# A decoder layer on one core: how the 308 keys of a head group are divided for the attention's second product

## The chip, the cores and the metric

The program runs on one core of a Trainium2 chip. The metric is the time of one execution on the device, in microseconds; lower is better. TensorE does the matrix products and the transposes, and writes them to PSUM. ACT (ScalarE) and DVE (VectorE) read PSUM, POOL (GpSimd) works on SBUF alone, and SP issues the DMAs.

## The reference

Eight sequences of 512 tokens of width 512 pass a layer of three parts, each with a residual and a layer norm. The first mixes tokens with FFTs over the head dimension and a cumulative sum. The third is a linear layer with int4-rounded weights and a low-rank part. The change is in the second, cross-attention over 77 context keys:

```python
q = _split_heads(queries @ W_q + b_q)          # 16 heads of 32
k = _split_heads(keys @ W_k + b_k)
v = _split_heads(values @ W_v + b_v)
scores = jnp.einsum('bhqd,bhkd->bhqk', q, k) / jnp.sqrt(jnp.float32(d))
scores = jnp.where(mask == 0, jnp.float32(-1000000.0), scores)
attn = jax.nn.softmax(scores, axis=-1)
out = jnp.einsum('bhqk,bhkd->bhqd', attn, v)
return out @ W_o + b_o
```

All is float32. The kernel keeps that precision by splitting each operand x in a high part (x rounded to the type float32r) and the rest, and by adding three products: high times high, low times high, high times low.

## The kernel before

The program has three stages: weights are prepared, tokens are mixed for all eight batches, and `attend` does the attention and the last layer. `attend` is what the change touches.

**Heads in groups.** The 16 heads are taken as 4 groups (`GROUPS`) of 4 heads (`GH`). A group has 4 x 77 = 308 key columns (`GK`). `k_block` holds the keys of a group block-diagonally, so three matmuls give the scores of a group for 128 tokens: 128 rows (tokens) by 308 columns. `v_block` holds the values of a group in the same way: 308 rows by 128 columns. Since a product can contract at most 128 rows, the 308 are divided by `KC` in pieces of 103, 103 and 102.

**From scores to the second product.** For a tile of 128 tokens (t = 0 to 3), DVE masks the scores and finds the maxima (`softmax_top`), ACT takes the exponentials (`exponentials`), POOL multiplies with the inverse sums (`normalize_probs`). `turn_probs` transposes the result on TensorE: for each of the three pieces c, four transposes (one a group) into one PSUM bank, which is called P{t}{c}. `split_probs` on ACT copies the bank as high part to `pT_hi`, `split_probs` on DVE subtracts it from the bank and writes `pT_lo`, and frees the bank. `weigh_values` then does, for each group g, 3 pieces x 3 products = 9 matmuls of 512 columns (all tokens of the batch) into bank V{g}. It is written for a batch in the step of the next batch.

**Loading the values.** The values are computed in batch 0's step and go to DRAM (`values_split`, from `store_values`). `load_values` brings those of a batch back into `v_block`. `v_pieces` gives the parts: a head's 77 keys are cut where a piece of `KC` ends, so there are 6 parts, of 77, 26, 51, 52, 25 and 77 rows, each for the high and the low half: 12 DMAs of rows x 4 groups x 32 columns. POOL clears `v_block` once at the start.

**What sets the order.** Each engine runs an order written out by hand: the function `step` in each engine's part, a start (batch 0), a loop over batches 2 to 6 with step 1 before it, a step for batch 7 and one for what is left. A step scores batch i, weighs the values of batch i-1, then interleaves the output projection (O0 to O3), the FFN (T and F) of batch i-1, and the transposes and query projection (X and Q) of batch i+1. All of it but the scores shares four PSUM banks in a ring, in the order of `BANK_ORDER` (`START_ORDER`, `CLOSING_ORDER`, `END_ORDER` at the ends): a use waits until the one four places ahead is freed, which the semaphore `freed` counts. The functions named `split_x1`, `split_q`, `split_o`, `split_x2`, `split_v` split their banks as `split_probs` does. SP's queue, too, is in one order; in the start it is: two stores of values, `load_values(0)`, two stores, the keys of batch 1, the weights of the output projection and FFN, the last store, the residual of batch 1's first norm. The residual load waits until the last store of values has landed.

In the rows, `x_tok` is also the buffer of the residual (`res1`), and of the values before they are stored; `xT_and_qT` is shared by several tiles. L62 is the helper that issues the three products, L1345 the transposes of the probabilities, L1852 `split_probs` on DVE, L1574 on ACT, L1824 the splits of `split_o` and `split_q`, L1816 those of `split_x1` and `split_x2`, L1892 the adding of a residual, L1216 the value loads, L566 the key loads, L1237 the stores of values.

## Time and profile before

| | us |
|---|---|
| median of 3 runs | 952.46 |
| range of the runs | 952.28 to 957.01 |
| the profiled execution | 953.44 |
| its span in the trace | 951.6 |
| TensorE (PE) busy | 902.9 (95%) |
| weight loads (PEld) busy | 748.9 (79%) |
| DVE busy | 667.3 (70%) |
| ACT busy | 376.3 (40%) |
| POOL busy | 336.1 (35%) |

The attention part begins at about 463 us of the span. Busy time is that of an engine's instructions; a weight load overlaps the matmul before it. For matmuls, which are pipelined, the distance from start to start is the cost, not the length of the record. An idle time in brackets is what an instruction's engine stood still before it, with the name of what it waited for.

### The profile page before, as it was taken

The page shows a single profiled execution, that of the slowest core. Times are in us where ns is not written, and L with a number is a line of the kernel's source. Part 1 is how long each engine was busy: PE and PEld are TensorE (multiplying, and loading weights), DVE is VectorE, ACT ScalarE, POOL GpSimd, SP SyncE. Part 2 cuts the span into 40 slices and gives each one's busy share as a digit, 9 for nine tenths or more (in the row PEclk, how much of TensorE's full clock was granted, in tenths as well). Part 3 has the DMA queues.
Part 4 walks back from the last instruction along what each step waited for, and adds up shares of the span by engine and source line. Part 5 has one row for each costly group of instructions (what it writes and reads, how often), then busy time and mean ns, then how long its engine had stood idle before and what let it go on. Part 6 is the DMA issues. An engine that isn't in the chain of part 4 may idle for free.

```text
span 951.6 us, 14736 instructions
## 1 busy us (share of the span) xinstructions
PE 902.9 (95%) x4472; PEld 748.9 (79%) x4472; DVE 667.3 (70%) x1128; ACT 376.3 (40%) x1414; POOL 336.1 (35%) x312
## 2 busy tenths in 40 slices
PE   7847999999999999999699999999999999999997
PEld 7726888888888888888588888888888888888775
DVE  3762465666565666567666987979788797887957
ACT  5621211111111111101485656756567556666611
POOL 0230525252424342426421433314244151431703
PEclk9988999999999999999999999999999999999999
DMA  9795204040404121214747332220312214020021
GB/s 308 254 352 195 89 12 166 11 166 18 160 34 142 44 89 45 89 45 153 263 139 253 111 93 64 81 76 21 120 34 90 67 24 136 13 90 22 16 78 44
DMA packets 91996, 100.09 MB, mean 105 GB/s; under 512 B 42824, under 2 KB 49224, under 8 KB 91952
## 3 DMA queue, kind: packets, MB, share of 16 engines
q1 hardware_dynamic: 91951, 99.55, 31.8%
q8 instruction: 22, 0.36, 0.2%
q14 instruction: 23, 0.18, 0.1%
HBM read 60.50 MB, written 39.03 MB: 105 GB/s over the span
## 4 chain that ended last, share of the span: by engine, by line
PE 42%; DMA 3%; DVE 2%; POOL 2%; issue 1%; ACT 1%; SPq 0%; POOLq 0%; DVEq 0%
PE shared_ps L62 32%; PE score_ps L62 4%; PE shared_ps L1345 4%; PE shared_ps L1308 1%; DMA values_split<-x_tok 1%; PE shared_ps L1378 1%; POOL probs L1726 1%; DMA w_o_and_ffn<-weights_split 1%; DMA x_tok<-residual_between 1%; DVE x_and_res L1914 0%; DVE xT_and_qT L1816 0%; ACT probs L1567 0%; POOL x_and_res L1735 0%; DVE y L1892 0%; POOL rstd L1719 0%
## 5 line engine op out<-in xcount | busy, mean ns | idle before, releaser
L1567 ACT ACTIVATE probs<-score_ps,top_s 128x77 f32<-128x77 f32 x512 | 158.9, 360 | 27.9 <-DVE top_s L1873 27.7
L1726 POOL TENSOR_TENSOR probs<-probs,per_total 128x616 f32<-128x616 f32 x64 | 83.2, 1317 | 116.2 <-DVE per_total L1880 116.1
L1567 ACT ACTIVATION_READ_ACCUMULATOR probs<-score_ps,top_s 128x1 f32 x512 | 124.2, 243 | 0.0
L62 PE MATMUL shared_ps<-w_o_and_ffn,xT_and_qT 128*128 128x512 f32 x384 | 96.7, 400 | 4.5 <-DVE xT_and_qT L1816 3.8
L1719 POOL TENSOR_TENSOR rstd<-ve,half_power 128x1 f32<-128x1 f32 x64 | 42.2, 660 | 163.3 <-DVE ve L1903 158.8
L62 PE MATMUL shared_ps<-w_o_and_ffn,xT_hi 128*128 128x512 f32 x256 | 88.2, 407 | 2.1 <-DVE xT_lo L1824 1.8
L62 PEld LDWEIGHTS shared_ps<-w_o_and_ffn,xT_and_qT 128*128 128x128 f32 x384 | 70.1, 188 | 21.6 <-DVE xT_and_qT L1816 4.1
L840 POOL TENSOR_TENSOR mix_rstd<-mix_ve,half_power 128x1 f32<-128x1 f32 x32 | 22.1, 689 | 154.9 <-DVE mix_ve L971 154.9
L788 ACT ACTIVATE v_sb<-v_ps 128x512 f32<-128x512 f32 x32 | 18.6, 594 | 142.0 <-PE v_ps L62 142.0
L1574 ACT ACTIVATE pT_hi<-shared_ps 103x512 fp32r<-103x512 f32 (+1 forms) x96 | 54.6, 609 | 42.7 <-PE shared_ps L1345 42.1
L62 PE MATMUL out_ps<-w_back_hi,xT_and_qT 128*128 128x512 f32 x224 | 71.0, 398 | 0.0
L62 PE MATMUL score_ps<-xT_and_qT 128*128 128x308 f32 x384 | 64.8, 311 | 5.8 <-ACT probs L1567 3.9
L795 ACT ACTIVATE xT_and_qT<-vals 128x512 fp32r<-128x512 f32 x32 | 19.4, 631 | 126.0 <-POOL vals L849 110.2
L62 PEld LDWEIGHTS score_ps<-xT_and_qT 128*128 128x128 f32 x384 | 58.3, 191 | 9.1 <-ACT probs L1567 4.1
L1852 DVE TENSOR_TENSOR pT_lo<-shared_ps,pT_hi 103x512 fp32r<-103x512 f32 (+1 forms) x96 | 64.7, 685 | 0.2 <-ACT pT_hi L1574 0.2
L849 POOL TENSOR_TENSOR vals<-qs_prod 128x512 f32<-128x512 f32 x32 | 41.0, 1293 | 54.7 <-DVE qs_prod L952 54.7
L62 PEld LDWEIGHTS shared_ps<-w_o_and_ffn,xT_hi 128*128 128x128 f32 x256 | 48.9, 191 | 14.0 <-issue 2.8
L1868 DVE COPY_PREDICATED score_ps<-hidden,masked 128x616 f32<-128x616 int32 x64 | 56.4, 882 | 4.8 <-PE score_ps L62 4.5
L1735 POOL TENSOR_TENSOR x_and_res<-x_and_res,bias_f 128x512 f32<-128x512 f32 x32 | 42.2, 1320 | 36.5 <-DVE x_and_res L1914 23.7
L1345 PE MATMUL shared_ps<-ident,probs 128*103 128x128 f32 (+1 forms) x384 | 52.3, 273 | 1.9 <-POOL probs L1726 1.9
L1873 DVE TENSOR_REDUCE top_s<-score_ps 128x8 f32<-128x616 f32 x64 | 51.2, 800 | 3.6
L963 DVE TENSOR_TENSOR mix_r<-out_ps,x_res 128x512 f32<-128x512 f32 x29 | 20.1, 691 | 47.0 <-PE out_ps L62 47.0
(199 smaller groups left out, 2303.6 us busy)
## 6 DMA issues: line engine op xcount, KB each, us to landing
...
x_between<-mix_x SPq DMA_DIRECT2D x32, 256.0 KB, 2.1
residual_between<-mix_res SPq DMA_DIRECT2D x32, 256.0 KB, 2.1
...
out<-y_out SPq DMA_DIRECT2D x32, 256.0 KB, 2.0
...
```

What stands on the lines that cost most here:

```text
L62: last = nc.tensor.matmul(out, l, r, start=(n == 0), stop=(n == len(terms) - 1))
L840: nc.gpsimd.tensor_tensor(rstd[:, t % 2:t % 2 + 1], ve[:, t % 2:t % 2 + 1], half_power[:], ALU.pow).then_inc(rstd_ready, 1)
L849: nc.gpsimd.tensor_tensor(vals[:, h, :], qs[:, 2 * h, :], qs[:, 2 * h + 1, :], ALU.subtract if h else ALU.add).then_inc(vals_summed, 1)
L1345: last = nc.tensor.transpose(shared_ps[s.bank(use)][0:size, g * P:(g + 1) * P], probs[:, t % 2, g * GK + at:g * GK + at + size], ident[:])
L1567: nc.scalar.activation(probs[:, t % 2, j * KEYS:(j + 1) * KEYS], score_ps[:, g, k * KEYS:(k + 1) * KEYS], ACT.Exp, bias=top[:, t % 2, j:j ...
L1574: nc.scalar.activation(pT[0][0:size, c, :, t * P:(t + 1) * P], turned_bank(s, t, c), ACT.Copy).then_inc(turned_hi, 1)
L1719: nc.gpsimd.tensor_tensor(rstd[:, n:n + 1], ve[:, n:n + 1], half_power[:], ALU.pow).then_inc(rstd_ready, 1)
L1726: nc.gpsimd.tensor_tensor(p, p, per_total[:, t % 2, h * heads:(h + 1) * heads].unsqueeze(2) .to_broadcast([P, heads, KEYS]), ALU.mult).the ...
L1735: nc.gpsimd.tensor_tensor(res2[:, t % 2, :], x2[:, t % 2, :], bias_f[:], ALU.add).then_inc(res2_ready, 1)
L1852: nc.vector.tensor_tensor(pT[1][0:size, c, :, tok], turned_bank(s, t, c), pT[0][0:size, c, :, tok].bitcast(F32), ALU.subtract).then_inc(fr ...
L1868: nc.vector.copy_predicated(s4, hidden[:, t, :].unsqueeze(1).unsqueeze(1).to_broadcast(shape), masked[:].unsqueeze(1).unsqueeze(1).to_broa ...
L1873: nc.vector.tensor_reduce(top[:, t % 2, h * 8:(h + 1) * 8].rearrange("p (g j) -> p g j", j=GH), s4, AX.X, ALU.max, negate=True).then_inc(t ...
```

## The change

The pieces of a group become 122, 122 and 64. In groups 0 and 2 the 64 are the last columns (244 to 307), in groups 1 and 3 the first (0 to 63). So the 64 of group 0 and the 64 of group 1 are neighbours in `probs`, and one transpose of 128 columns turns both: the rows 0 to 63 of its result belong to the even group, the rows 64 to 127 to the odd one. `turn_probs` has four transposes in the first bank (both 122s of groups 0 and 1) and four in the second (those of groups 2 and 3), and two in the third.

In the third bank ACT copies the high parts of the even and of the odd groups in two instructions, each to its own 64 rows of a new tile `pT_tail`. DVE writes the low parts, again in two instructions, to the other 64 rows of the same group's column block. So `pT_tail[:, g]` has the high part in one half of its rows and the low part in the other. `v_tail[0]` has the high part of the values in both halves, `v_tail[1]` the low part only beside the high part of the probabilities. Two products then do what three did. The two DVE instructions count on a semaphore of their own, `tail_lo`; DVE waits for both and adds one to `freed` itself.

The value loads follow: `v_pieces` has 10 parts (77, 45, 32, 77, 13 rows for the even groups, 13, 77, 32, 45, 77 for the odd ones), each for two of the four groups, for high and low half, and three DMAs of 64 rows for each parity fill `v_tail`: 26 in place of 12.

```diff
-KC = [(0, 103), (103, 103), (206, 102)]
+TAIL = 64
+CHUNK = (GK - TAIL) // 2
+
+MAIN = [[0, CHUNK], [TAIL, TAIL + CHUNK]]
...
-    for j in range(GH):
-        for c, (at, size) in enumerate(KC):
-            a, b = max(j * KEYS, at), min((j + 1) * KEYS, at + size)
-            if a < b:
-                yield j, c, a - at, a - j * KEYS, b - a
+    for odd in range(2):
+        for j in range(GH):
+            for c, at in enumerate(MAIN[odd]):
+                a, b = max(j * KEYS, at), min((j + 1) * KEYS, at + CHUNK)
+                if a < b:
+                    yield odd, j, c, a - at, a - j * KEYS, b - a
+
+
+V_LOADS = 2 * len(list(v_pieces())) + 6
...
             def load_values(i):
 
                 wait_reuse(sp, oT_hi, i * NC)
+                src = [v_dram[part].rearrange("r (g j d) -> r g j d", g=GROUPS, j=GH) for part in range(2)]
                 for part in range(2):
-                    src = v_dram[part].rearrange("r (g j d) -> r g j d", g=GROUPS, j=GH)
-                    for j, c, row, key, n in v_pieces():
-                        sp.dma_start(v_block[part][row:row + n, c, :, j * XHD:(j + 1) * XHD].bitcast(F32),
-                                     src[bass.ds(i * KEYS + key, n)][:, :, j, :]).then_inc(v_loaded, 16)
+                    for odd, j, c, row, key, n in v_pieces():
+                        sp.dma_start(v_block[part][row:row + n, c, odd:GROUPS:2, j * XHD:(j + 1) * XHD].bitcast(F32),
+                                     src[part][bass.ds(i * KEYS + key, n)][:, odd:GROUPS:2, j, :]).then_inc(v_loaded, 16)
+                for odd, j, key in ((0, GH - 1, KEYS - TAIL), (1, 0, 0)):
+                    for part, half in ((0, 0), (0, 1), (1, odd)):
+                        sp.dma_start(v_tail[part][64 * half:64 * (half + 1), odd:GROUPS:2, j * XHD:(j + 1) * XHD].bitcast(F32),
+                                     src[part][bass.ds(i * KEYS + key, TAIL)][:, odd:GROUPS:2, j, :]).then_inc(v_loaded, 16)
...
-            sp.wait_ge(values_cleared, 2)
+            sp.wait_ge(values_cleared, 4)
...
-                at, size = KC[c]
-                for g in range(GROUPS):
-                    last = nc.tensor.transpose(shared_ps[s.bank(use)][0:size, g * P:(g + 1) * P],
-                                               probs[:, t % 2, g * GK + at:g * GK + at + size], ident[:])
+                if c < 2:
+                    for k in range(2):
+                        for g in range(2):
+                            at = (2 * c + g) * GK + MAIN[g][k]
+                            last = nc.tensor.transpose(shared_ps[s.bank(use)][0:CHUNK, (2 * k + g) * P:(2 * k + g + 1) * P],
+                                                       probs[:, t % 2, at:at + CHUNK], ident[:])
+                else:
+                    for k in range(2):
+                        at = (2 * k + 1) * GK - TAIL
+                        last = nc.tensor.transpose(shared_ps[s.bank(use)][:, k * P:(k + 1) * P],
+                                                   probs[:, t % 2, at:at + 2 * TAIL], ident[:])
...
+                out = shared_ps[s.bank(use)][:]
+                terms = [(v_block[a][:, c, g, :], pT[b][:, c, g, :]) for c in range(2) for a, b in ((0, 0), (1, 0), (0, 1))]
+                for n, (l, r) in enumerate(terms):
+                    nc.tensor.matmul(out, l, r, start=(n == 0), stop=False)
+
+                nc.tensor.matmul(out, v_tail[0][:, g, :], pT_tail[:, g, :], start=False, stop=False)
+                nc.tensor.matmul(out, v_tail[1][:, g, :], pT_tail[:, g, :], start=False, stop=True).then_inc(filled, 1)
...
+                    psum, (hi, lo) = turned_main(s, t, c)
+                    nc.scalar.activation(hi, psum, ACT.Copy).then_inc(turned_hi, 1)
...
+                else:
+                    for odd in range(2):
+                        psum, (hi, lo) = turned_tail(s, t, odd)
+                        nc.scalar.activation(hi, psum, ACT.Copy).then_inc(turned_hi, 1)
...
+                    dve.wait_ge(turned_hi, nth(i, NT * 4, 4 * t + 3))
+                    psum, (hi, lo) = turned_tail(s, t, 0)
+                    nc.vector.tensor_tensor(lo, psum, hi.bitcast(F32), ALU.subtract).then_inc(tail_lo, 1)
+                    psum, (hi, lo) = turned_tail(s, t, 1)
+                    nc.vector.tensor_tensor(lo, psum, hi.bitcast(F32), ALU.subtract).then_inc(tail_lo, 1)
+                    dve.wait_ge(tail_lo, nth(i, NT * 2, 2 * t + 1))
+                    dve.sem_inc(freed, 1)
```

**SP, start of the attention part: `load_values(0)` and the stores after it.** In the names, `values_split` is the DRAM buffer; rows x groups x columns. Before:

```order
L1216 DMA v_block_hi<-values_split 77x4x32 [waits x1_stored1,v_stored0,v_stored1,x1_stored0,values_cleared]
L1216 DMA v_block_hi<-values_split 26x4x32
L1216 DMA v_block_hi<-values_split 51x4x32
L1216 DMA v_block_hi<-values_split 52x4x32
L1216 DMA v_block_hi<-values_split 25x4x32
L1216 DMA v_block_hi<-values_split 77x4x32
```

and the same six for the low half. Of the change:

```order
L1231 DMA v_block_hi<-values_split 77x2x32 [waits x1_stored1,v_stored0,v_stored1,x1_stored0,values_cleared]
L1231 DMA v_block_hi<-values_split 45x2x32
L1231 DMA v_block_hi<-values_split 32x2x32
L1231 DMA v_block_hi<-values_split 77x2x32
L1231 DMA v_block_hi<-values_split 13x2x32 x2
L1231 DMA v_block_hi<-values_split 77x2x32
L1231 DMA v_block_hi<-values_split 32x2x32
L1231 DMA v_block_hi<-values_split 45x2x32
L1231 DMA v_block_hi<-values_split 77x2x32
L1235 DMA v_tail_hi<-values_split 64x2x32 x2
L1235 DMA v_tail_lo<-values_split 64x2x32
```

The ten of `v_block` come again for the low half, the three of `v_tail` for the odd groups. Twelve issues have become 26; behind them, unmoved, follow the stores, keys, weights and the residual.

**DVE, in a step, around the split of token tile 0's third bank, up to the next maxima.** `stats`, `mv` and `ve` belong to the layer norm, `top_s` to the softmax. Before:

```order
L1901 BN_AGGR mv<-stats 128x2 [waits stat_done]
L1903 TENSOR_SCALAR ve<-mv 128x1 [waits aggr_done]
L1852 TENSOR_TENSOR pT_lo<-shared_ps,pT_hi 102x4x128 [waits pT_hi_ready]
L1868 COPY_PREDICATED score_ps<-hidden,masked 128x2x308 [waits scored,hidden_ready]
L1873 TENSOR_REDUCE top_s<-score_ps 128x8 [waits exped,hid]
```

Of the change:

```order
L1942 BN_AGGR mv<-stats 128x2 [waits stat_done]
L1944 TENSOR_SCALAR ve<-mv 128x1 [waits aggr_done]
L1890 TENSOR_TENSOR pT_tail<-shared_ps,pT_tail 64x2x128 [waits pT_hi_ready]
L1892 TENSOR_TENSOR pT_tail<-shared_ps,pT_tail 64x2x128
L1909 COPY_PREDICATED score_ps<-hidden,masked 128x2x308 [waits tail_lo,scored,hidden_ready]
L1914 TENSOR_REDUCE top_s<-score_ps 128x8 [waits exped,hid]
```

One instruction of 512 columns has become two of 256 with fewer rows, and what stands behind them waits for them (`tail_lo`).

**TensorE, `weigh_values` of one group.** Before, nine matmuls, three times:

```order
L62 MATMUL shared_ps<-pT_hi,v_block_hi 128x512 [waits pT_hi_ready,shared_freed,v_loaded]
L62 MATMUL shared_ps<-pT_hi,v_block_lo 128x512
L62 MATMUL shared_ps<-pT_lo,v_block_hi 128x512
```

Of the change, the like of these twice (L1385), and then:

```order
L1387 MATMUL shared_ps<-pT_tail,v_tail_hi 128x512
L1388 MATMUL shared_ps<-pT_tail,v_tail_lo 128x512
```

Nothing else on TensorE moves, but the third transposes of each tile, of which two are left of four.

## Rows read from the trace of the kernel before

**Rows 1.** One stretch of an ordinary step: length, busy us and instructions, PEclk, DMA.
```profile
626.50:685.00 58.50, 57.93 (x311) 49.23 (x310) 48.90 (x91) 35.35 (x156) 20.48 (x20) 1.00 0.23 67
```

**Rows 2.** Waits of the weight loads, 440 to 952: total us, times, longest.
```profile
PEld shared_ps L1345 <- DVE xT_lo L1816: 0.9, 5, 0.2
```

**Rows 3.** Timeline of TensorE and DVE in that step: start, us, instruction, [idle before].
```profile
650.53 3.06 PE L62 MATMUL shared_ps<-w_o_and_ffn,xT_and_qT 128*128 128x512 f32 x12 [0.57 <-DVE xT_and_qT L1816]
663.44 0.65 PE L1345 MATMUL shared_ps<-ident,probs 128*102 128x128 f32 x4
...
648.28 0.69 DVE L1892 TENSOR_TENSOR y<-shared_ps,x_tok 128x512 f32<-128x512 f32 x1
...
662.09 1.29 DVE L1816 TENSOR_TENSOR xT_lo<-shared_ps,xT_hi 128x512 fp32r<-128x512 f32 x2
```

**Rows 4.** The chain that ended last, 460 to 545: start, us, what.
```profile
509.39 11.19 DMA values_split<-x_tok
...
520.59 5.59 DMA x_tok<-residual_between
...
534.18 3.04 PE shared_ps L62 x12
```

**Rows 5.** Timeline of SP's queue in the start.
```profile
487.56 5.29 SPq L1216 DMA_DIRECT2D v_block_hi<-values_split  x6
...
497.99 2.75 SPq L1237 DMA_DIRECT2D values_split<-x_tok  x4
500.79 3.82 SPq L566 DMA_DIRECT2D xT_and_qT<-keys_split  x8
```

**Rows 6.** Timeline of TensorE: end of the values, first output projection, last transposes.
```profile
636.81 0.39 PE L62 MATMUL shared_ps<-pT_lo,v_block_hi 102*128 102x512 f32 x1
637.04 1.86 PE L62 MATMUL score_ps<-xT_and_qT 128*128 128x308 f32 x12
638.84 0.49 PE L62 MATMUL shared_ps<-w_o_and_ffn,xT_hi 128*128 128x512 f32 x1
...
681.25 1.47 PE L1345 MATMUL shared_ps<-ident,probs 128*103 128x128 f32 x12
682.47 0.48 PE L62 MATMUL shared_ps<-xT_hi,w_q_hi 128*128 128x512 f32 x1
```

**Rows 7.** Timeline of ACT and DVE: the splits of the weighed values.
```profile
636.13 0.80 ACT L1580 ACTIVATE xT_hi<-shared_ps,bias_v 128x512 fp32r<-128x512 f32 x1
637.24 0.69 ACT L1580 ACTIVATE xT_hi<-shared_ps,bias_v 128x512 fp32r<-128x512 f32 x1 [0.30 <-PE shared_ps L62]
...
637.96 0.75 DVE L1824 SCALAR_TENSOR_TENSOR xT_lo<-shared_ps,bias_v,xT_hi 128x512 fp32r<-128x512 f32 x1 [0.24 <-ACT xT_hi L1580]
```

**Rows 8.** Groups by form: busy us, mean ns of one; last, a wait for itself.
```profile
L1852 DVE TENSOR_TENSOR pT_lo<-shared_ps,pT_hi 102x512 fp32r<-102x512 f32 x32 | 21.8, 682 | 0.0
...
L440 DVE TENSOR_TENSOR xT_and_qT<-side,xT_and_qT 128x208 fp32r<-128x208 f32 x2 | 0.7, 366 | 0.0
...
L474 DVE TENSOR_TENSOR xT_and_qT<-turned,xT_and_qT 16x512 fp32r<-16x512 f32 x1 | 0.7, 683 | 0.0
...
643.84 0.18 DVE L1901 BATCH_NORM_AGGREGATE mv<-stats 128x2 f32<-128x6 f32 x1 [0.16 <-DVE stats L1898]
```

**Rows 9.** Single value loads (51, 52, 77 rows), and us of a store to landing.
```profile
489.50 0.76 SPq L1216 DMA_DIRECT2D v_block_hi<-values_split  x1
...
490.31 0.85 SPq L1216 DMA_DIRECT2D v_block_hi<-values_split  x1
...
492.02 0.83 SPq L1216 DMA_DIRECT2D v_block_hi<-values_split  x1
...
values_split<-x_tok SPq DMA_DIRECT2D x8, 256.0 KB, 2.2
```

**Rows 10.** Timeline of TensorE: first score and first output projection of step 1.
```profile
510.11 1.01 PE L62 MATMUL score_ps<-xT_and_qT 128*128 128x308 f32 x6
...
522.11 0.47 PE L62 MATMUL shared_ps<-w_o_and_ffn,xT_hi 128*128 128x512 f32 x1 [0.16 <-issue]
```

39 lines of the change are left out of this document (20 added, 19 removed).

## The prediction

> **What bounds the kernel now.** I read the stretches first, then the waits, then single engines in order of time. In one ordinary batch step of the attention part TensorE is busy 57.93 of 58.50 us at a granted clock of 1.00, and DVE 48.90 [rows 1]. So a matmul less should be time less. Two things qualify this. In each step TensorE stops once for 0.57 us before the FFN of the first token tile, and DVE is what it waits for [rows 3]. And a little later there is a place without slack: over the loop, the weight load of the transposes P12 (probabilities of token tile 1, third bank) waits for DVE's `xT_lo` five times, 0.9 us in sum [rows 2]. Between the two DVE runs in one piece: it begins at 648.28, when the third output projection is filled, and the pair of `xT_lo` that releases P12 starts at 662.09 and takes 1.29; TensorE starts P12 at 663.44 [rows 3]. That is 15.2 us of a step in which DVE sets the pace and TensorE only follows. In the rest of the step TensorE does.
>
> At the start of the attention part the bound is another one. The chain of waits goes through the DMAs: the last store of values is issued at 509.39 and lands 11.19 us later, behind the weights; the load of the residual for the first output projection follows at 520.58 and takes 5.59; DVE adds it, and that ends in the FFN matmuls at 534.18 [rows 4]. Ahead of it SP issues without a pause: two times six value loads, four stores, eight key loads [rows 5]. Whatever is put into that row of issues moves the residual.
>
> **TensorE: what is removed.** Per token tile 12 transposes become 10. Twelve take from 681.25 to the next product at 682.47, 1.22 us, so 0.10 each [rows 6]; 0.20 per tile. Per group of values 9 matmuls become 8. V3's last matmul starts at 636.81 and the score behind it at 637.04 [rows 6]: 0.23 each, 0.92 per batch. A batch gives 4 x 0.20 + 0.92 = 1.72 us on TensorE, eight batches 13.8.
>
> **How much of the 0.92 arrives.** After V3 TensorE does two scores (637.04) and starts the output projection at 638.84 [rows 6], since it needs V3 split. ACT is in the way: its split of V2 starts at 636.13, as soon as the exponentials are through, and V3's at 637.24, having waited 0.30 for TensorE [rows 7]. With V3 done 0.92 earlier, at 636.3, ACT is still at exponentials and V2. These start earlier only by the one matmul that V0 and V1 are each shorter (about 0.2), so ACT takes V3 at about 636.6 and DVE, 0.67 apart from V2's, ends at 638.2 in place of 638.7 (it starts at 637.96 and takes 0.75 [rows 7]). The output projection moves by 0.50 and the other 0.42 are waited.
>
> **DVE: what is added.** The third piece of a tile was one TENSOR_TENSOR of 682 ns [rows 8]; now it is two of 64x256, which the rows do not have. 128x208 takes 366 and 16x512, as few rows as that, 683 [rows 8], so rows do not count and columns do: 48 more columns at (682 - 366) / 304 = 1.04 ns make 416. Back to back a record overlaps the next by 0.09, so the pair costs 0.65 where one cost 0.59: +0.07. Then DVE waits for its own results and adds one to `freed`. The same pattern (wait on itself, then an increment) stands in the norm: aggregate waits 0.16 idle for stats [rows 8], and the overlap of 0.09 is lost too: +0.25. Bounds are 0.04 and 0.35; I take 0.25, as the pattern is the same. Sum +0.32 per tile. Queued behind that wait are the masking of the next scores (tile 0), a split of queries, a norm. For tile 0 it stands inside the 15.2 us, so all of it arrives at P12: +0.32. For tiles 1 and 2 DVE has over 0.5 us in hand where TensorE needs it next. For tile 3 it comes just ahead of the next batch's V0, where 0.1 is lost. ACT's pair of halves is about as much dearer (+0.07) but ACT sits idle next to each.
>
> **Sum of an ordinary step.** Tile 0's transposes: 0, since TensorE waits for DVE there anyway (0.57 becomes 0.77). P12 late +0.32. Tiles 1, 2, 3: -0.60. V0 +0.10. V part -0.50. Sum -0.68. Other waits have little slack too (the bank for the last query projection), for which I allow 0.15, an estimate of a quarter of the gain: **-0.53 per step** instead of -1.72. Cover: what hides nothing is TensorE's; if DVE were not on the chain, the whole 1.72 came out.
>
> **SP: the added issues.** A batch's values come in 26 DMAs, not 12. Two times six took 487.56 to 497.99, 10.43 us, 0.87 each with the gap [rows 5]. Their issue takes 0.83 for 77 rows, 0.85 for 52 and 0.76 for 51 [rows 9]; key loads of 32 rows, with the same three-level pattern, take 3.82 us for eight, 0.48 apart [rows 5]. Which price do the new shapes have? Of the 26, sixteen have 77, 45 or 13 rows, ten have 32 or 64. I price the sixteen like the old value loads (0.87) and the ten like key loads (0.48), as they are nearest by rows: 13.9 + 4.8 = **18.7 us, +8.3**. Ends: all at 0.48 (the pattern now has 2 groups in place of 4) 12.5, +2.1; all at 0.87 22.6, +12.2.
> By the Trainium skill, page "DMA: Bandwidth & Descriptors", section "Why a DMA increments its semaphore by 16 and not by 1", a transfer runs on the largest number of DMA engines up to 16 that divides its slowest dimension, and the sequencer itself writes the semaphore counts of the rest. By that rule 32 and 64 rows fall in with the key loads and 45 and 13 do not, which is my split; the trace agrees in that 32 rows go 0.48 apart and 77 and 52 rows take 0.83 and 0.85, but 51 rows, by the rule those with the most to write, take 0.76.
>
> In an ordinary step this hides: TensorE reads the values a step later, and the output store queued behind waits for nothing that DVE needs before the third tile. In batch 0 it does not hide. SP has 0.95 us in hand there (four stores take 2.75 [rows 5], four issues of 0.45 would take 1.8), so keys and weights go 7.35 later. Before them, ACT's split of the last values needs the third store landed: issued at 506.8 in the new order, 2.2 to land [rows 9], 509.0. From there follow that split, two more banks (together 2.9, an estimate from splits of 0.6 to 0.7 by ACT and DVE each [rows 7, 8], partly side by side) and the last query projection (12 x 0.23 = 2.8): the first score of step 1 starts at 514.7 in place of 510.11 [rows 10]. That would cost 4.6, but the other path is later: weights issued at 512.0, last store of values landed at 527.9, residual at 533.5 in place of 526.18 [rows 4]. From its landing to the FFN DVE is busy in one piece, so TensorE reaches the FFN at 541.5 instead of 534.18: **+7.35**. What batch 0 and V of batch 1 save before that is waited away.
>
> **Sum.** Start +7.35. Rest of step 1: +0.32 - 0.60 + 0.25 = -0.03. Steps 2 to 7: 6 x -0.53 = -3.18. Last step: V alone, without exponentials in ACT's way, -0.92. Total +3.2. The profiled execution took 953.44 (span 951.6), 0.98 over the median of the three runs; so 956.6 against its own time, and against the median, 952.46, 955.7. What a measurement here can tell from no change is about 0.5%, 4.8 us: below 947.7 or above 957.2.
>
> **The rivals.** (1) *TensorE alone sets the steps*, DVE gives way: the waits at P12 are only 0.9 us in five [rows 2], so some slack might appear there, and the DVE stretch holds instructions slowed by neighbours. Then step 1 gives -0.60 and six steps 1.72 each, the last 0.92: 7.35 - 0.6 - 10.3 - 0.9 = -4.5, 948.0. Against it: DVE has no idle row between 648.28 and 662.09 beyond waits for itself. (2) *Cheap issues*: half as many runs per DMA make all 26 cost 0.48: start +1.1 (2.1 less 0.95), total -3.0, 949.5. With (1) as well, -10.7, 941.8. (3) *Slower than before*: the issues of the value loads ahead of the residual. If the 32- and 64-row loads cost 0.87 as well, the start costs 11.25 and the total is +7.1, 959.6. The place is SP's row of issues in batch 0, the price 0.39 more for ten issues; it decides from about 20 us for the 26 issues on. (4) *The change does not do what it says*: halves at other partitions, or a wait dearer than in the norm, cost DVE 0.7 more per step in its stretch: a step gives +0.17, step 1 +0.67, total +8.1, 960.6.
>
> **Chances.** Forecast 0.42 (own range 953 to 958.5); (1) 0.17; (2) 0.13; (1) and (2) together 0.03; (3) 0.17; (4) 0.08. The 80% range reaches from rival 1 to (3) and (4): 946.5 to 961. Faster by over 0.5%: half of rival 1 and the joint case, with what noise adds, 0.13. Slower by over 0.5%: (3), (4) and a quarter of the forecast, 0.35. The same: 0.52.
>
> **What would show it.** Right: SP's first batch of value loads takes 18 to 19 us; 32- and 64-row loads are short issues and 45- and 13-row ones long; the residual lands about 7 us later and DVE's first add of an output projection waits 4 or more for it; a step's period is about 57.8 in place of 58.4 (the first output projections of steps 1 and 3 start at 522.11 and 638.84, 116.73 apart for two steps [rows 6, 10]); the wait before the first FFN tile grows from 0.57 to about 0.8; the halves take about 416 ns. Wrong in the steps: a period under 57.2 (rival 1) or over 58.5 (4). Wrong at the start: issues done in under 15 or over 21 us.

## The result and the profile after

| | median | runs | ratio to before |
|---|---|---|---|
| before | 953.22 us | 6 (952.28 to 957.01) | |
| after | 966.61 us | 6 (964.59 to 967.71) | 1.0133, 95% [1.0113, 1.0153] |
| predicted | 955.7 us | range 946.5 to 961.0 | |

The change makes the kernel 1.3% slower, 12.7 us by the ratio. The forecast was +3.2; the sign of its likeliest case was right, the size was not, and the time lies outside the range. The profiled execution of after took 967.71 us.

In the page of after TensorE is busy 4 us less and DVE 13 us more (667.3 in the page of before), over a span 14 us longer:

```profile
span 965.9 us, 14884 instructions
...
PE 898.9 (93%) x4376; PEld 737.6 (76%) x4376; DVE 680.7 (70%) x1160; ACT 381.2 (39%) x1446; POOL 330.0 (34%) x314
```

**The start.** SP's queue in the changed kernel, the place of [rows 5] (start, us, instruction). L1231 and L1235 are the value loads of the main chunks and of the tails:

```profile
490.57 8.73 SPq L1231 DMA_DIRECT2D v_block_hi<-values_split  x10
499.34 8.23 SPq L1231 DMA_DIRECT2D v_block_lo<-values_split  x10
507.62 1.24 SPq L1235 DMA_DIRECT2D v_tail_hi<-values_split  x2
...
511.49 2.06 SPq L1256 DMA_DIRECT2D values_split<-x_tok  x4
513.59 3.84 SPq L573 DMA_DIRECT2D xT_and_qT<-keys_split  x8
```

The 26 loads take 20.9 us where twelve took 10.43 [rows 5]. The chain behind them is the one of [rows 4], moved as a whole (chain of waits; start, us, what; the last line is DVE's add, from its timeline):

```profile
522.25 11.24 DMA values_split<-x_tok
533.50 5.47 DMA x_tok<-residual_between
539.07 0.70 DVE y L1933
```

From the landing of the residual to the first FFN tile it takes 8.0 us in both. That tile starts at 546.96 instead of 534.18 [rows 4]. The +12.8 divides into 3.0 by which the loads begin later (chance, as K shows below), 10.5 for their issue, and 0.7 that the four stores behind them (2.06 against 2.75) give back. So 9.8 of it belong to the change.

**The steps.** The first FFN tile of steps 2 and 3, and P12, the third-bank transposes of token tile 1 (timeline of TensorE; the first row ends with its window, inside the tile):

```profile
604.82 2.37 PE L69 MATMUL shared_ps<-w_o_and_ffn,xT_and_qT 128*128 128x512 f32 x9 [0.79 <-DVE xT_and_qT L1850]
...
663.10 3.06 PE L69 MATMUL shared_ps<-w_o_and_ffn,xT_and_qT 128*128 128x512 f32 x12 [0.78 <-DVE xT_and_qT L1850]
...
676.72 0.44 PE L1371 MATMUL shared_ps<-ident,probs 128*128 128x128 f32 x2
```

The two FFN tiles are 58.28 apart, as in the kernel before. So TensorE's saving of 1.7 us a step is gone whole. In this step TensorE is busy 56.7 of the 58.3 us, in the kernel before 57.7, so 1.0 of it stands there as idle time; the rest is in gaps that this sum doesn't show. For the stretch 590 to 840, the waits of TensorE in the changed kernel (total us, times, longest), where before has only the first of these with 2.9 us:

```profile
PE shared_ps L69 <- DVE xT_and_qT L1850: 3.9, 5, 0.8
PE shared_ps L69 <- DVE xT_lo L1858: 1.4, 5, 0.3
PE shared_ps L69 <- DVE y L1933: 1.1, 4, 0.3
PE shared_ps L1385 <- DVEq L1894: 0.8, 4, 0.2
```

All four releasers are on DVE; the last is the line with the increment behind DVE's wait on itself. And what DVE does there (its timeline, tile 0):

```profile
663.93 0.15 DVE L1944 TENSOR_SCALAR ve<-mv 128x1 f32<-128x1 f32 x1
664.12 0.42 DVE L1890 TENSOR_TENSOR pT_tail<-shared_ps,pT_tail 64x256 fp32r<-64x256 f32 x1
664.57 0.43 DVE L1892 TENSOR_TENSOR pT_tail<-shared_ps,pT_tail 64x256 fp32r<-64x256 f32 x1
665.37 0.81 DVE L1909 COPY_PREDICATED score_ps<-hidden,masked 128x616 f32<-128x616 int32 x1 [0.37 <-DVE pT_tail L1892]
```

From `ve` to the mask it is 1.44 us. In the kernel before the same two stand 0.71 apart:

```profile
651.38 0.15 DVE L1903 TENSOR_SCALAR ve<-mv 128x1 f32<-128x1 f32 x1
651.48 0.69 DVE L1852 TENSOR_TENSOR pT_lo<-shared_ps,pT_hi 102x512 fp32r<-102x512 f32 x1
652.09 0.80 DVE L1868 COPY_PREDICATED score_ps<-hidden,masked 128x616 f32<-128x616 int32 x1
```

### The profile page after: what moved, and what is told of

It reads as the page before. It is cut to its first block, busy times and chain, and to the rows that moved or that the text cites. A ratio compares the mean times of both kernels' runs of the same rounds, so it can differ in the third digit from the quotient of the medians.

```text
span 965.9 us, 14884 instructions
## 1 busy us (share of the span) xinstructions
PE 898.9 (93%) x4376; PEld 737.6 (76%) x4376; DVE 680.7 (70%) x1160; ACT 381.2 (39%) x1446; POOL 330.0 (34%) x314
## 4 chain that ended last, share of the span: by engine, by line
PE 29%; DVE 8%; ACT 4%; issue 4%; SPq 3%; DMA 3%; DVEq 0%; POOLq 0%; POOL 0%; ACTq 0%
PE shared_ps L69 22%; ACT probs L1597 3%; PE score_ps L69 2%; SPq L1231 2%; DMA values_split<-x_tok 1%; PE shared_ps L1366 1%; DVE score_ps L1909 1%; DVE y L1933 1%; PE shared_ps L1327 1%; DVE stats L1939 1%; DMA w_o_and_ffn<-weights_split 1%; PE shared_ps L1408 1%; ACT xT_hi L1614 1%; PE shared_ps L1385 1%; DVE xT_lo L1858 1%
## 5 line engine op out<-in xcount | busy, mean ns | idle before, releaser
L1753 POOL TENSOR_TENSOR rstd<-ve,half_power 128x1 f32<-128x1 f32 x64 | 38.4, 600 | 166.0 <-DVE ve L1944 165.9
L69 PEld LDWEIGHTS score_ps<-xT_and_qT 128*128 128x128 f32 x384 | 58.1, 190 | 10.4 <-ACT probs L1597 5.5
L1909 DVE COPY_PREDICATED score_ps<-hidden,masked 128x616 f32<-128x616 int32 x64 | 59.6, 931 | 6.2 <-PE score_ps L69 3.6
L1605 ACT ACTIVATE pT_hi<-shared_ps 122x512 fp32r<-122x512 f32 x64 | 37.1, 615 | 39.6 <-PE shared_ps L1366 38.7
L69 PE MATMUL shared_ps<-w_o_and_ffn,xT_lo 128*128 128x512 f32 x128 | 50.7, 396 | 0.0
L69 PEld LDWEIGHTS out_ps<-w_back_hi,xT_and_qT 128*128 128x128 f32 x224 | 41.6, 188 | 9.6
```

Source lines behind the costliest of these rows:

```text
L69: last = nc.tensor.matmul(out, l, r, start=(n == 0), stop=(n == len(terms) - 1))
L1605: nc.scalar.activation(hi, psum, ACT.Copy).then_inc(turned_hi, 1)
L1753: nc.gpsimd.tensor_tensor(rstd[:, n:n + 1], ve[:, n:n + 1], half_power[:], ALU.pow).then_inc(rstd_ready, 1)
L1909: nc.vector.copy_predicated(s4, hidden[:, t, :].unsqueeze(1).unsqueeze(1).to_broadcast(shape), masked[:].unsqueeze(1).unsqueeze(1).to_broa ...
```

## The experiments

All times are medians beside runs of before on the same chip (953.4 to 954.7); the ratio has its 95% interval. "Period" is the distance from one step's first FFN tile to the next one's in the profile, the typical one of steps 2 to 6. In the kernel before it is 58.28, in the changed kernel 58.28.

| kernel | us | ratio | period |
|---|---|---|---|
| K before again | 954.2 | 1.0008 [0.9990, 1.0026] | 58.26 |
| A 12 more issues, batch 0 | 963.7 | 1.0087 [1.0058, 1.0115] | 58.23 |
| E 12 more issues, later batches | 953.8 | 1.0007 [0.9995, 1.0020] | 58.22 |
| B after, start reordered | 961.4 | 1.0059 [1.0038, 1.0080] | 58.34 |
| R after, 14 loads | 957.3 | 1.0038 [1.0020, 1.0056] | 58.29 |
| D TensorE's saving alone | 948.2 | 0.9920 [0.9897, 0.9942] | 57.12 |
| H DVE's halves and wait alone | 957.6 | 1.0048 [1.0029, 1.0066] | 58.79 |
| P both | 951.1 | 0.9970 [0.9953, 0.9987] | 57.74 |
| Q P and ACT's halves | 949.5 | 0.9959 [0.9944, 0.9973] | 57.75 |
| T1 Q, halves on different rows | 952.4 | 0.9989 [0.9966, 1.0012] | 57.97 |
| T2 T1, results moved to other rows | 954.7 | 1.0008 [0.9992, 1.0025] | 58.17 |
| C after without the wait | 964.3 | 1.0102 [1.0083, 1.0122] | 57.94 |
| G unstacked, 64-row matmuls | 971.9 | 1.0204 [1.0176, 1.0231] | 59.04 |
| GB G, start reordered | 970.3 | 1.0180 [1.0161, 1.0200] | 59.03 |
| M unstacked, 128-row matmuls | 960.6 | 1.0089 [1.0063, 1.0115] | 57.58 |
| N M with 12 loads | 951.5 | 0.9973 [0.9958, 0.9988] | 57.60 |
| S N, start shortened | 950.7 | 0.9970 [0.9954, 0.9986] | 57.56 |

### The start

**A, E.** `load_values` of before, each load in two; in A for batch 0, in E for all others:

```
-sp.dma_start(v_block[part][row:row + n, c, :, j * XHD:(j + 1) * XHD].bitcast(F32),
-             src[bass.ds(i * KEYS + key, n)][:, :, j, :]).then_inc(v_loaded, 16)
+for odd in range(2) if isinstance(i, int) and i == 0 else [None]:
+    groups = slice(0, GROUPS) if odd is None else slice(odd, GROUPS, 2)
+    sp.dma_start(v_block[part][row:row + n, c, groups, j * XHD:(j + 1) * XHD].bitcast(F32),
+                 src[bass.ds(i * KEYS + key, n)][:, groups, j, :]).then_inc(v_loaded, 16)
```

> The kernel before with one thing changed: each of the 12 value loads of batch 0, ahead of step 1, is cut in two (groups 0 and 2, groups 1 and 3), the same bytes in 24 loads. Theory SP (the loss of the change is the time that SyncE takes to issue loads at the start, 0.82 to 0.87 us for each whatever its rows): 12 more issues x 0.83 = +10.0, less some 0.7 of slack, so +9 us in all, 962 us; the residual lands 10 us later, and the first FFN tile starts 9 us later. Rival (a halved load is issued in 0.44 us, as the 64-column ones of the tails suggest): +5.3 - 0.7 = +4.6. Rival (the loss is DVE's and the stacking's, the start's issues are hidden): 0.

> The kernel before with the value loads of batches 1 to 7 cut in two (24 instead of 12) and those of batch 0 left whole, the counterpart of A_start_issues. Theory (in the steps SyncE is idle most of the time, its issues lie beside the rest): within 1 us of before, 953 to 954.5, period 58.3. Rival (every issue costs, for instance since the next batch's keys and the stores stand behind them): up to +9 us a step.

A: +9.0 us by the medians (8.3 by the ratio), as the SP theory said. Its queue (x12 are the loads of one half):

```profile
490.84 10.30 SPq L1218 DMA_DIRECT2D v_block_hi<-values_split  x12
501.19 10.09 SPq L1218 DMA_DIRECT2D v_block_lo<-values_split  x12
```

E: no difference. Twelve more loads cost 9.0 us together, 0.75 each, where the next thing waits for them, and nothing in a step.

**R.** With high and low rows side by side in DRAM one load fetches both; 14 loads instead of 26, the rest as in the changed kernel:

```
-    v_dram = nc.dram_tensor("values_split", (2, B * KEYS, D), F32).ap()
+    v_dram = nc.dram_tensor("values_split", (B * KEYS, 2, D), F32).ap()
...
-                src = [v_dram[part].rearrange("r (g j d) -> r g j d", g=GROUPS, j=GH) for part in range(2)]
+                src = v_dram.rearrange("r a (g j d) -> r (a g) j d", g=GROUPS, j=GH)
```

> The changed kernel with the high and low values of a key side by side in DRAM, so that one load fetches both: 14 value loads a batch instead of 26, everything else as in the changed kernel, stacking and wait too. Theory (of the changed kernel's 12 to 13 us, 9 are the start's issues and the rest the end and chance): the start's loads take 11.5 us, 9 us less than in the changed kernel, and the whole is at 956 to 959, 3 to 5 us over before, with a period of 58.3. Rival (the start's delay comes from the stacked tiles, not from the issues): 965.

957.3, inside what was expected. The stacking, the wait and the period are those of the changed kernel, and 9.1 us of its loss (by the ratios) are gone. So about 9 of the 12.7 us are the issues of twelve loads at the start; R still has two more than the kernel before.

**B.** The order of SP's start:

```
-                sp.wait_ge(v_stored[n], 32)
-            load_values(0)
+            sp.wait_ge(v_stored[0], 32)
+            load_values(0, 0)
             store_values(2)
+            load_values(0, 1)
             store_values(3)
+            load_values(0, 2)
             load_next_keys(1)
+            store_values(4)
```

The second argument says which part (high, low, tails). Behind it come `w_o`, the residual, then `w_ffn`.

> The changed kernel with SyncE's start in another order: batch 0's values need the first stored tile alone, so its loads begin behind that store, and the stores of tiles 2, 3 and 4 are issued as soon as their tile is split instead of behind all 26 value loads; the residual goes ahead of the FFN weights. Nothing else differs. Theory SP: the 6.0 us in which TensorE waited for the split of tile 3, whose slot the late store held, and the late residual go: some 9 to 11 us below the changed kernel, 956 to 958 us; what is left over 953 is the end of the program. Rival (the stacked steps themselves cost more, DVE): at most 2 us less than the changed kernel, 965.

5.2 us less than the changed kernel by the medians, 7 by the ratios, where 9 to 11 were expected. The late store is no longer waited for (6.0 us in the changed kernel), but the keys of batch 1, which stand behind the same loads, are (waits of TensorE, 440 to 962; total us, times, longest):

```profile
PE score_ps L69 <- DMA xT_and_qT<-keys_split: 3.8, 1, 3.8
```

The queue is full from 484 to 518 us. An order can choose who waits; only fewer or cheaper issues shorten it.

**K.** The 3.0 us by which the loads of after began late:

> The kernel before, unchanged, for a second profile of it. The changed kernel's value loads of batch 0 began 3.0 us later than in the first profile of before (490.6 against 487.6), though nothing ahead of them was changed. Theory (that 3.0 us is chance, of the matmuls on the context at a lower granted clock): the loads begin at 490 to 491 here too, the first FFN tile of step 1 at 537, the period of a step is 58.3. Rival (the change itself delays them): they begin at 487.6 again. Ratio 1.00.

K's loads began at 487.05, as the rival had it, and yet the change isn't what delays them: A, which is the kernel before up to that point, began at 490.84. Over all profiles with this order of the start, in the eleven of the kernel before and kernels made from it they began at 487.05 to 491.57 (mean 489.0), in the six of the changed kernel and kernels made from it at 487.29 to 491.06 (mean 489.1). So the delay comes and goes without the change. Where it comes, TensorE has waited longer for the loads of the first value product (2.94 us in A, 1.69 in K), and the granted clock is then down for a part of the stretch to the lower of its two levels, 1.2 GHz: that product takes 4.57 in A, 3.02 in K. A and then K (start and end, length, TensorE busy, clock, DMA share, GB/s):

```profile
475.00:480.00 5.00, 2.74 (x7) 0.72 0.97 352
```

```profile
475.00:480.00 5.00, 5.00 (x30) 1.00 0.84 294
```

**F.** Behind the end of the kernel before, loads of eleven shapes, one at a time (one run, 1024.5 us with them):

```
+            sp.dma_start(spare[0:77], v_dram[0].rearrange("r (g j d) -> r g j d", g=GROUPS, j=GH)[0:77, :, 0]).then_inc(spare_loaded, 16)
+            sp.wait_ge(spare_loaded, 16)
```

> The kernel before, and behind its end 33 further loads of parts of the stored values into a spare tile, one at a time, each behind the landing of the one before: eleven shapes, each three times (77, 80, 128, 64, 32, 16 and 13 rows, with 4 runs or 2 runs of 32 columns a row, and 77 rows with one run of 128 columns). It tells what the 0.82 to 0.87 us of a value load's issue, the 0.60 of a tail's and the 0.48 of a key's go with. Theory (a load has one price whatever its rows, but 64 rows are divided among the 16 engines without a rest): 64, 80, 128, 32 and 16 rows at 0.6, 77, 45 and 13 rows at 0.83. Rival (the price goes with the count of runs): 77x4 the dearest, 16x4 and 13x2 under 0.5. The program is some 70 us longer by it.

One of the three turns, in the order 77 rows x 4 runs, 45 x 2, 32 x 2, 13 x 2, 80 x 4, 16 x 4, and 77 rows with one run of 128 columns (min/median/max ns):

```profile
L1300 SPq DMA_DIRECT2D spare<-values_split x1: 848/848/848, 951.0 to 951.0; - x1
...
L1304 SPq DMA_DIRECT2D spare<-values_split x1: 849/849/849, 955.7 to 955.7; - x1
...
L1306 SPq DMA_DIRECT2D spare<-values_split x1: 647/647/647, 958.0 to 958.0; - x1
...
L1308 SPq DMA_DIRECT2D spare<-values_split x1: 849/849/849, 960.0 to 960.0; - x1
...
L1314 SPq DMA_DIRECT2D spare<-values_split x1: 599/599/599, 966.3 to 966.3; - x1
...
L1318 SPq DMA_DIRECT2D spare<-values_split x1: 599/599/599, 970.8 to 970.8; - x1
...
L1320 SPq DMA_DIRECT2D spare<-values_split x1: 350/350/350, 972.7 to 972.7; - x1
```

Rows that 16 divides are issued in 0.56 to 0.65 us, the others of this run in 0.82 to 0.86, 80 rows cheaper than 77 and 77 as dear as 13, as the theory said; the number of runs hardly matters until the row is one run, which costs 0.32 to 0.35. Sixteen loads of the dear kind (0.84), ten of the cheap one (0.61) and 0.04 between two make 20.6 of the changed kernel's 20.9 us.

By the Trainium skill, page "DMA: Bandwidth & Descriptors", section "Why a DMA increments its semaphore by 16 and not by 1", a transfer runs on the largest number of DMA engines up to 16 that divides its slowest dimension, here the rows, and the sequencer writes the semaphore counts of the others. The two prices fall as that division does. But the counts left over don't order the dear ones: 45 rows, which leave one by that rule, take 0.85 to 0.88 in the changed kernel (once 1.09), 25 and 51 rows, which leave 11 and 13, take 0.76 to 0.77 in the kernel before. What the 0.2 us between the two kinds are is open.

### The steps

**D.** In `turn_probs` and `weigh_values` of before:

```
-                for g in range(GROUPS):
+                for g in range(GROUPS if c < 2 else 2):
...
+                terms = [(l[a], r[b]) for l, r in pieces for a, b in ((0, 0), (1, 0), (0, 1))][:8]
```

> The kernel before with TensorE's saving alone: of the third bank only two of the four transposes are made, and of each value bank the last of the nine matmuls is left out, so part of the attention is left out; DVE, ACT and the loads are as before. Theory (the chain DVE to ACT to TensorE sets the value part, TensorE sets the rest): the 8 transposes give 0.6 per step and the value part 0.1 to 0.4 of its 0.92: 0.7 to 1.0 a step, 5 to 8 us in all, 945 to 948. Rival (TensorE alone sets the steps): 1.7 a step and 0.9 in the last, 13 us in all, 940. Rival (DVE alone sets them): 0 to 1 us.

-6.5 us and 1.16 a step, a little more of a step than expected. TensorE alone doesn't set the steps (1.7 was there to be had), but two thirds of its saving arrive when DVE is left as it is. The changed kernel has the same saving and a period of 58.28; it loses 1.16 against D. The next runs divide that.

**H, P, Q.** On DVE, and in Q in the same way on ACT:

```
+for k in range(2):
+    nc.vector.tensor_tensor(pT[1][0:size, c, 2 * k:2 * k + 2, tok], turned_bank(s, t, c)[:, 2 * k:2 * k + 2],
+                            pT[0][0:size, c, 2 * k:2 * k + 2, tok].bitcast(F32),
+                            ALU.subtract).then_inc(half_lo, 1)
+dve.wait_ge(half_lo, nth(i, NT * 2, 2 * t + 1))
+dve.sem_inc(freed, 1)
```

> The kernel before with DVE's part of the change alone: the low part of the third bank is made in two halves of 256 columns (102 rows each), behind them DVE waits for both and only then frees the bank; matmuls, ACT and loads are as before. Theory (the halves and the wait take back what TensorE gives, 1.15 us a step by the periods of 58.27 in the changed kernel and 57.12 with TensorE's saving alone): +0.8 to +1.2 a step, +6 to +9 us in all, 961 to 963. Rival (the step's end is set by TensorE in other stretches, so DVE's loss shows only where TensorE's gain is): 0 to +2 us, 955 to 957. The prediction's own term was +0.32 a step, +2.5 us.

> The kernel before with TensorE's saving (D_pe_only: two transposes of the third bank and one matmul of each value bank left out) and DVE's part (H_dve_only: two halves, a wait, then the free) together; ACT and the loads as before. D alone gave a period of 57.12, H alone 58.79, before has 58.28. Theory (with TensorE faster the DVE halves cost more than the 0.51 they cost alone, since DVE now sets the value part as well; they account for nearly all that the changed kernel loses against D): 58.0 to 58.3, 952 to 955. Rival (the costs are plain sums, and the rest of the changed kernel's loss is ACT's halves): 57.6, 949.

> P_pe_and_dve with ACT's part added: the high part of the third bank is made in two operations of 256 columns as well, and DVE's first half waits for both, as in the changed kernel; two transposes and a value matmul in nine are left out as there. Theory (ACT's second half makes DVE's halves, and with them the exponentials and the value part, later: the 0.53 us a step that is left of the changed kernel's loss against D_pe_only): a period of 58.1 to 58.3, 3 to 4 us above P_pe_and_dve, 954 to 955. Rival (ACT is idle there and the 0.53 comes from the 122-row transposes and banks): 57.75, 951.

H: +0.51 a step, half of what I expected then, 0.2 more than the prediction's term. P: +0.62 on top of D. It lies between its two answers and near the second: the costs are nearly plain sums. Q: nothing, so ACT's halves cost nothing and that theory fell. 0.53 a step stayed open.

**C.** The changed kernel, each half frees the bank itself and such a bank counts as two:

```
-    dve.wait_ge(tail_lo, nth(i, NT * 2, 2 * t + 1))
-    dve.sem_inc(freed, 1)
...
+    return sum(2 if u[0] == "P" and u[2] == "2" else 1 for u in uses)
```

> The changed kernel without DVE's wait on itself behind the two halves of the tail: each half frees the bank by itself, and the counts of freed banks are two for such a bank. Theory (the wait holds DVE's sequencer, so that the mask operation behind it starts 0.37 us late and later waits are not met ahead): 0.25 to 0.37 us less for each of the 4 tiles on DVE, of which the periods show 0.5 per step: 3 to 4 us below the changed kernel, 962.5 to 963.5. Rival (DVE's wait lies beside other work): the same time, 966.5.

0.34 less a step (0.5 was expected), and in all 2.3 us less by the medians, 3.0 by the ratios, at or under the low end of the range. The wait costs 0.35 on DVE, 1.09 from `ve` to the mask instead of 1.44:

```profile
661.93 0.15 DVE L1950 TENSOR_SCALAR ve<-mv 128x1 f32<-128x1 f32 x1
662.11 0.87 DVE L1900 TENSOR_TENSOR pT_tail<-shared_ps,pT_tail 64x256 fp32r<-64x256 f32 x2
663.02 0.81 DVE L1915 COPY_PREDICATED score_ps<-hidden,masked 128x616 f32<-128x616 int32 x1
```

Of the 0.34, 0.32 arrive at P12 (13.30 behind the first FFN tile instead of 13.62).

**T1, T2.** In Q the halves have 102 rows each, all read from row 0 on. In the changed kernel the second is read from row 64 on, and both are written to the other 64 rows. T1 gives Q's halves rows 0 to 63 and 64 to 101; T2 also writes them to the other half:

```
-for k, rows, to in ((0, slice(0, 64), slice(0, 64)),
-                    (1, slice(64, size), slice(64, size))):
+for k, rows, to in ((0, slice(0, 64), slice(64, 128)),
+                    (1, slice(64, size), slice(0, size - 64))):
```

> Q_pe_dve_act with DVE's two halves cut to 64 and 38 rows, written to the rows that they are read from; the rest of the low part is left as it is, so part of the attention is left out. Control for T2. Theory (the count of rows doesn't matter to DVE, only the columns): as Q_pe_dve_act, two halves in 0.75 us, a period of 57.75, 949 to 951.

> T1_rows_kept with the results written to the other half of the rows (rows 0 to 63 to 64 to 127, rows 64 to 101 to 0 to 37), as the changed kernel's stacking does. Theory (a result that moves to other rows can't overlap with the operation before or behind it): the halves take 0.42 us each and start at least 0.03 behind the end of the one before, 0.2 us more for each tile, a period of 58.1 to 58.3, 3 to 4 us above T1. Rival (the 0.53 is the changed kernel's own tiles and banks, the tail's tile shared by ACT and DVE for one): as T1, 57.75.

T1's theory fell: it isn't Q's time, but 0.22 a step more. T2 adds another 0.20, a period inside its theory's range; in time it adds 2.4 us by the medians, less than the 3 to 4 expected. The two from `ve` on, Q and then T2 (T2's second half has 38 rows; a merged row shows the shape of its first):

```profile
650.72 0.15 DVE L1917 TENSOR_SCALAR ve<-mv 128x1 f32<-128x1 f32 x1
650.82 0.75 DVE L1863 TENSOR_TENSOR pT_lo<-shared_ps,pT_hi 102x256 fp32r<-102x256 f32 x2
651.94 0.81 DVE L1882 COPY_PREDICATED score_ps<-hidden,masked 128x616 f32<-128x616 int32 x1 [0.37 <-DVE pT_lo L1863]
```

```profile
658.03 0.15 DVE L1918 TENSOR_SCALAR ve<-mv 128x1 f32<-128x1 f32 x1
658.22 0.87 DVE L1864 TENSOR_TENSOR pT_lo<-shared_ps,pT_hi 64x256 fp32r<-64x256 f32 x2
659.46 0.81 DVE L1883 COPY_PREDICATED score_ps<-hidden,masked 128x616 f32<-128x616 int32 x1 [0.37 <-DVE pT_lo L1864]
```

In Q the first half starts 0.10 behind the start of `ve`, which takes 0.15: they overlap. In T2 it starts when `ve` is over. The way from `ve` to the mask is 0.71 in before, 1.22 in Q, 1.35 in T1, 1.43 in T2, 1.44 in the changed kernel. So of its +0.73, 0.51 are two halves and the wait, 0.13 the second half on other rows than the first, 0.08 the results on other rows than the sources. The rows of Q divide the 0.51: the pair takes 0.75 where one operation took 0.69, DVE then stands idle 0.37, and the 0.08 by which the mask overlapped the operation before it are lost. T1's first half has 64 rows and takes the same 0.42 as Q's 102, so it isn't the count of rows. TensorE meets this at two places of a step: from Q to T2 P12 starts 0.19 later behind the first FFN tile (13.42 and 13.61), and V0 0.24 later behind the score ahead of it (0.95 and 1.19), which is how 0.21 on DVE becomes 0.42 in the period. By the Trainium skill, page "VectorE: DVE Perf Modes", section "Two Vector instructions with no wait between them", a DVE instruction is held until all earlier ones have finished when its first row lies in another group of 32 than that of the last read, or of the last write, in the same memory. That names in Q none, in T1 the second half, in T2 and the changed kernel both; the trace agrees, at about 0.1 us each.

### What the stacking is good for, and a faster kernel

**G, GB.** The shared transposes without the stacking: one ACT and one DVE operation of 128 rows x 256 columns for the tail bank, high and low in tiles of their own, and for each group

```
-nc.tensor.matmul(out, v_tail[0][:, g, :], pT_tail[:, g, :], start=False, stop=False)
-nc.tensor.matmul(out, v_tail[1][:, g, :], pT_tail[:, g, :], start=False, stop=True).then_inc(filled, 1)
+rows = slice(64 * (g % 2), 64 * (g % 2 + 1))
+for a, b in ((0, 0), (1, 0), (0, 1)):
+    last = nc.tensor.matmul(out, v_tail[a][rows, g, :], pT_tail[b][rows, g // 2, :], start=False, stop=(b == 1))
```

> The changed kernel with the shared transposes of the 64s but without the stacking: the tail bank (128 rows, 256 columns) is split by one ACT operation into a high tile and by one DVE operation into a low tile, and each group's value bank takes three matmuls on its own 64 rows (9 in all, as before), 24 value loads instead of 26. Theory (stacking costs DVE more than its one matmul saves): DVE has 256 columns less per tile than before and no wait on itself, TensorE keeps the 8 transposes' saving, 0.6 a step: a period of 57.3 to 57.7, 4 to 7 us below the changed kernel in the steps and 1 us in the start, 959 to 962. Rival (TensorE's ninth matmul costs what the stack saved): period 58.2, 965.

> The same with SyncE's start in the other order (values of batch 0 behind the first store, later stores between the pieces, residual ahead of the FFN weights). Theory: both gains add, 5 us below G_unstacked, 954 to 957, about the kernel before or a little under. Rival (the start of step 1 is held by the 24 loads whatever their order): as G_unstacked.

Both were far off: 971.9 and 970.3. The way to the values was D's (V0 34.95 behind the first FFN tile, D 34.88), but the value part took 10.7 us instead of 9.1. TensorE in the first value bank (L1384 the 122-row matmuls, L1388 the 64-row ones):

```profile
697.10 0.39 PE L1384 MATMUL shared_ps<-pT_lo,v_block_hi 122*128 122x512 f32 x1
697.42 0.49 PE L1388 MATMUL shared_ps<-pT_tail_hi,v_tail_hi 64*128 64x512 f32 x1
697.76 0.39 PE L1388 MATMUL shared_ps<-pT_tail_hi,v_tail_lo 64*128 64x512 f32 x1
697.99 0.39 PE L1388 MATMUL shared_ps<-pT_tail_lo,v_tail_hi 64*128 64x512 f32 x1
698.31 1.12 PE L69 MATMUL score_ps<-xT_and_qT 128*128 128x308 f32 x6
```

Matmuls of one size start 0.23 apart. Where 122 rows turn to 64, the starts are 0.32 and then 0.34 apart: 0.2 more for each such change, two changes a bank, eight a batch: the 1.6 us.

**M.** The same three matmuls on all 128 rows, with zeros for the other group's values.

> G_unstacked with one thing changed: the three tail matmuls of each value bank contract all 128 rows, against values that are zero in the other group's half, instead of the group's own 64 rows. Theory (in G_unstacked each change between a 122-row and a 64-row matmul cost TensorE 0.1 us on both sides of it, 0.39 us per bank, 1.5 us a step): the value part is 9.1 us again, the period 57.5 to 57.7, 10 us below G_unstacked, 961 to 963, of which 8 to 9 over before are the 24 loads at the start and 4 to 5 under it the steps. Rival (that extra time is the wait for the tail's low part, whose rows come late): as G_unstacked, 972.

960.6, 11.4 us below G, the period 57.58: confirmed. The stacking avoids the same price by filling the 128 rows, but so do zeros, and then DVE needs one operation, no move and no wait.

**N, S.** M with R's layout, 12 loads; S also with one store for each tile's high and low values and a shorter start.

> M_padded with the high and low values of a key side by side in DRAM, so that one load fetches both: 12 value loads instead of 24, each with 4 runs of 32 columns a row. Theory (the issue price is per load, 0.83 us, whatever its columns): the start's loads take 10 us as in the kernel before, the first FFN tile starts where it does there, 533 to 537, and with a period of 57.5 to 57.7 the kernel is at 948 to 950, 4 to 5 us below before. Rival (the price goes with the bytes or runs of a load): the loads take 18 us and the time stays at M_padded's.

> N_padded_12_loads with SyncE's start shortened: one store for each tile's high and low values instead of two, batch 0's loads behind the first store alone, the last store ahead of the weights and the residual ahead of the FFN weights. Theory (the start of step 1 is still held by SyncE's queue: 2.5 us of waiting for w_o and the late residual in N_padded_12_loads): 2 to 4 us below it, 947 to 949.5. Rival (the rest of the start is set by ACT and TensorE): the same as N_padded_12_loads, 951.

N: 951.5, ratio 0.9973, a gain over before that the runs can tell, though smaller than expected: its loads take 10.4 us as in before, but of the 4 to 5 us that 0.7 a step should give only 2 to 3 are there. In its profile the steps give 3.3 and the last two 0.6, and the loads begin 3.5 us later than in before, by the chance that K shows; what the other executions lost was not divided. S isn't told apart from N. Its residual is issued 13.4 us earlier (510.67 against 524.08), and still the first FFN tile starts only 1.8 earlier. The wait for weights that its expectation meant to remove (2.5 in N, 2.8 in S) is that of the first value product, at 474 to 477, ahead of all value loads, as in before (1.7), and not one for `w_o`.

## Why the prediction was wrong

- **The start, +7.35: right in its mechanism, too small.** The chain was the one foretold: loads, last store, residual, DVE's add, FFN. The split into sixteen dear and ten cheap loads was right. The term that failed is the price of the ten: 0.48 apart, taken from the key loads, where the trace has 0.64 to 0.68 (0.60 to 0.64 each and the gap). With some dear ones over 0.87 too that is 20.9 us instead of 18.7. The slack behind was 0.7, not 0.95. So the start costs 9.8 instead of 7.35; twelve loads alone measured +9.0 (A) and, taken out, -9.1 (R). Rival 3, all 26 at 0.87 and a start of +11.25, was nearer, 1.5 too high where the forecast was 2.4 too low.
- **DVE, +0.32 a tile: this step failed.** The two halves and the wait cost 0.51, not 0.32 (Q). The pair's +0.07 was right (0.06). The wait, +0.25 with the lost overlap and taken from the norm (0.16 idle), was not: DVE stands idle 0.37 and loses 0.08 of overlap, 0.45 together, over the upper of its two bounds. What makes the norm's wait cheaper was not tested. The sentence that rows do not count is right for how long an operation takes and wrong for when it can start: the halves lie on other rows than their neighbours and than their own sources, which costs 0.2 more. Together +0.73 on DVE. Of this +0.71 arrive at P12: it starts 13.62 behind the first FFN tile, against 12.91 [rows 3].
- **Tile 3, "0.1 is lost": too small.** V0 starts 1.21 behind the score ahead of it, against 0.85 before: +0.36. TensorE waits 0.20 of it by name, for DVE.
- **The value part, -0.50: right.** From V0 to the first output projection it takes 10.47, before 10.93: -0.46. The output projection waits 0.28 for `xT_lo`.
- **The transposes of tiles 1 to 3, -0.60: right.** From P12 to the scores after P32 the changed kernel takes 21.27 us, before 21.89. Those of tile 0 gave nothing, as foretold: the wait ahead of the FFN grew from 0.57 to 0.78.
- **The sum of a step: 0.00 instead of -0.53.** +0.39 at P12 and +0.26 at V0 more than foretold; the 0.15 allowed for other waits is not there. Over the five periods that is 2.7 us. Rival 1 is refuted by D; rival 4 (DVE 0.7 dearer in its stretch, a step +0.17) named the right mechanism and nearly the size, with a chance of 0.08.
- **The last two steps, -0.53 and -0.92: this failed too.** The profiles show +0.5 and, where no stretch of low clock disturbs it, +1.15. From the first FFN tile of step 6 to that of step 7 the changed kernel takes 62.65, before 62.13; with TensorE's saving alone (D) it is 60.74, with DVE's part alone (H) 63.29. From there to the first FFN tile of the last step it takes 45.4 in B and R, 44.2 in A. In this stretch the values of batch 7 begin 24.2 us behind the first FFN tile (24.27 in the changed kernel), against 22.07 in A and 22.08 in before, and then take 9.3 instead of 10.2 to 10.3. So the -0.92 came, and 2.1 us ahead of it were lost, where TensorE waits mostly for DVE. H, with DVE's part alone, loses 1.0 there, but N, which has neither halves nor wait, loses as much; what makes up the 2.1 was not divided. First matmul of the values, the changed kernel and then A (first FFN tiles at 900.53 and 899.63):

```profile
924.80 0.39 PE L1385 MATMUL shared_ps<-pT_hi,v_block_hi 122*128 122x512 f32 x1
```

```profile
921.70 0.39 PE L62 MATMUL shared_ps<-pT_hi,v_block_hi 103*128 103x512 f32 x1
```

In the profiles of before and of the changed kernel these 44 to 45 us are 45.73 and 47.04, since the granted clock is down for a part of the output projections (0.66 at 920 to 925 in before, 0.69 at 935 to 940 in the changed kernel); A and B have no such stretch, so those 1.5 to 1.7 us are not the change's. A slow tile need not cost time, either. In the changed kernel one FFN tile takes 4.59, and the next still starts 6.48 behind its start; in B, the same kernel with another start, the tile takes 3.04 and the next starts 6.42 behind. The changed kernel, then B:

```profile
910.36 4.59 PE L69 MATMUL shared_ps<-w_o_and_ffn,xT_and_qT 128*128 128x512 f32 x12
...
916.84 3.04 PE L69 MATMUL shared_ps<-w_o_and_ffn,xT_and_qT 128*128 128x512 f32 x12 [0.80 <-DVE xT_and_qT L1850]
```

```profile
907.31 3.04 PE L69 MATMUL shared_ps<-w_o_and_ffn,xT_and_qT 128*128 128x512 f32 x12
...
913.73 3.04 PE L69 MATMUL shared_ps<-w_o_and_ffn,xT_and_qT 128*128 128x512 f32 x12 [1.27 <-DVE xT_and_qT L1855]
```

The first of them in its stretch:

```profile
910.00:915.00 5.00, 4.97 (x17) 0.66 0.09 34
```

**What stays open.** The start's 9.8, the steps' 0 and 1.65 for the last two make 11.5 of the 12.7 us (interval 10.8 to 14.6); for R the same sum is about 2.4 of 3.6 (1.9 to 5.3), since its 14 loads take 11.2 us, 0.8 more than the twelve did. So the rest is within what the runs can tell. A part of it may be clock: the mean granted clock was 0.977 to 0.980 in the six executions of the changed kernel and 0.980 to 0.987 in the 27 of before that stand beside R, whose own were 0.976 to 0.987. How many microseconds that is was not divided. The last 0.1 of the 1.16 us a step between T2 and the changed kernel is open as well.
